# A ternary feed-forward stage: quantisation factors from the maximum alone, the inverse root on GpSimd, and another order of work on three engines

## The reference

```python
xn = layernorm(x)
def bitlinear(x, w, b):                       # w1: 1024x256, w2: 256x1024
    r = rsqrt(mean(x*x, -1) + 1e-5)           # per token
    scale = 127 / clip(max|x*r|, 1e-5)        # per token
    q = clip(round(x*r*scale), -128, 127) / scale
    wq = clip(round(w / mean|w|), -1, 1) * mean|w|
    return q @ wq.T + b
x = x + bitlinear(gelu(bitlinear(xn, w1, b1)), w2, b2)
```

## Time and profile before

| | us |
|---|---|
| median of 3 runs (lowest, highest) | 1340.75 (1338.74, 1341.14) |
| the profiled execution's own time | 1341.27 |
| its span, first to last instruction | 1339.6 |
| busy over the span: TensorE, VectorE, ScalarE, GpSimd | 1058.0, 942.7, 761.9, 224.7 |
| mean granted TensorE clock, share of full speed | 0.873 |

### The profile page before, as it was taken

How to read it: one execution, slowest core, us unless ns; L and a number is a source line. 1 busy time by engine, 2 the same in 40 slices (tenths; PEclk the granted TensorE clock), 3 DMA queues, 4 the chain that set the end, 5 groups by cost and what they waited for, 6 DMA issues and landing times. The chain is left out here.

```text
span 1339.6 us, 28328 instructions
## 1 busy us (share of the span) xinstructions
PE 1058.0 (79%) x9218; PEld 862.1 (64%) x9218; DVE 942.7 (70%) x2613; ACT 761.9 (57%) x2799; POOL 224.7 (17%) x326
## 2 busy tenths in 40 slices
PE   3999946568999823556999978999988775598885
PEld 2788843246888612445677758999977675366664
DVE  3688877755888667774677755666657984489994
ACT  1688865657888626775677762121213331488884
POOL 1233200012222101001223210000002220233431
PEclk7799968758999956776999988999998886599998
DMA  6231000000000000002322000000000000000001
GB/s 216 63 110 53 15 1 0 0 9 13 17 12 16 2 0 1 0 0 82 74 71 71 12 1 1 0 0 0 1 16 17 16 16 1 0 2 1 0 0 64
DMA packets 44421, 32.58 MB, mean 24 GB/s; under 512 B 16184, under 2 KB 43456, under 8 KB 44352
## 3 DMA queue, kind: packets, MB, share of 16 engines
q1 hardware_dynamic: 44352, 31.72, 7.8%
HBM read 23.32 MB, written 2.10 MB: 19 GB/s over the span
## 5 line engine op out<-in xcount | busy, mean ns | idle before, releaser
L680 ACT ACTIVATE L1a_pr<-L1a_scores,L1a_nm 128x128 f32<-128x128 f32 x256 | 93.1, 417 | 4.2 <-DVE L1a_nm L738 3.5
L680 ACT ACTIVATE L2a_pr<-L2a_scores,L2a_nm 128x128 f32<-128x128 f32 x256 | 90.8, 393 | 5.4 <-DVE L2a_nm L738 5.4
L680 ACT ACTIVATE L0a_pr<-L0a_scores,L0a_nm 128x128 f32<-128x128 f32 x256 | 90.8, 393 | 3.8 <-DVE L0a_nm L738 3.8
L680 ACT ACTIVATE L3f_pr<-L3f_scores,L3f_nm 128x128 f32<-128x128 f32 x256 | 90.5, 403 | 3.3 <-DVE L3f_nm L738 3.3
L680 ACT ACTIVATION_READ_ACCUMULATOR L1a_pr<-L1a_scores,L1a_nm 128x1 f32 x256 | 65.3, 255 | 0.0
L680 ACT ACTIVATION_READ_ACCUMULATOR L3f_pr<-L3f_scores,L3f_nm 128x1 f32 x256 | 62.4, 244 | 0.0
L1533 PE MATMUL L2f_inner<-L2f_taT,L2f_loraBT 128*128 128x128 f32 x512 | 59.6, 275 | 0.0
L1596 ACT COPY L2f_xTb<-L2f_xT 128x256 f32<-128x256 f32 x16 | 6.4, 406 | 93.5 <-PE L2f_inner L1522 93.5
L738 DVE TENSOR_REDUCE L2a_nm<-L2a_scores 128x4 f32<-128x512 f32 x64 | 42.2, 683 | 24.4 <-PE L2a_scores L570 24.4
L680 ACT ACTIVATION_READ_ACCUMULATOR L2a_pr<-L2a_scores,L2a_nm 128x1 f32 x256 | 59.3, 231 | 0.0
L1522 PEld LDWEIGHTS L2f_inner<-L2f_xTb,L2f_wiT 128*128 128x128 f32 x512 | 58.8, 193 | 0.4
(11 more groups left out here) (524 smaller groups left out, 3182.8 us busy)
## 6 DMA issues: line engine op xcount, KB each, us to landing
setup_ctx_nat<-in_ctx SPq DMA_DIRECT2D x4, 512.0 KB, 5.5
x_all<-in_x SPq DMA_DIRECT2D x1, 2048.0 KB, 12.4
L0a_ctxT<-ctxT_all SPq DMA_DIRECT2D x16, 128.0 KB, 2.0
L_ffn_w<-in_L_ffn_w SPq DMA_DIRECT2D x2, 1024.0 KB, 6.1
L1a_ctxT<-ctxT_all SPq DMA_DIRECT2D x16, 128.0 KB, 2.0
L2a_ctxT<-ctxT_all SPq DMA_DIRECT2D x16, 128.0 KB, 2.0
L3a_mem<-in_ctx SPq DMA_DIRECT2D x16, 128.0 KB, 2.0
out<-x_all SPq DMA_DIRECT2D x1, 2048.0 KB, 7.5
```

Of the source, the lines that this page charges most:

```text
L680: ex = act.activation(pr[q.s][:, j, h, :], S[j][:, h * P:h * P + P], ACT.Exp, bias=nm[q.s][:, j, h:h + 1], scale=-1.0, accum_out=ls[q.s][: ...
```

## The change

1. `factors` is parted. `factor` makes the scaling factor from the maximum alone (clip, reciprocal: two tiny instructions instead of five). `dequant` for the first product is one instruction with the ready root. The dequantiser of the second product moves to GpSimd.
2. The inverse root of the second product (`RsqrtPool`): VectorE makes -v/2, the shift and the first guess (four tiny instructions), GpSimd the three Newton steps (12 dependent instructions on 128x2) and the product with the kept maximum.
3. VectorE's sweep has four pairs (`sweep_four`): norm, maximum and factor 0 are made for the pair after nxt, called far. Its step now begins with max|h| and factor 1 of cur and ends with the head of cur's root; the output of old waits for GpSimd's dequantiser.
4. A quarter of hqT (second stream, second half) is written by VectorE.
5. ScalarE's order: hs of old, gelu of cur, xs of nxt, first stream's hqT of old, xqT of nxt, the third quarter of hqT, squares of cur. TensorE's order: transposes of hs of old come ahead of those of xs of nxt, and each waits for the residual of the pair before.
6. GpSimd's stream is written out for all turns without a loop.

The diff, cut to its core:

```diff
+class RsqrtPool:
+    def vector(self, dve, src, scale, eps, i):
+        dve.tensor_scalar(v, src, scale, eps, ALU.mult, ALU.add).then_inc(self.s_v, 1)
+        dve.tensor_scalar(h, src, -0.5 * scale, -0.5 * eps, ALU.mult, ALU.add)
+        dve.wait_ge(self.s_v, i)
+        dve.tensor_scalar(j, v.bitcast(I32), 1, None, ALU.arith_shift_right).then_inc(self.s_j, 1)
+        dve.wait_ge(self.s_j, i)
+        dve.tensor_scalar(y.bitcast(I32), j, -1.0, float(0x5F3759DF), ALU.mult, ALU.add).then_inc(self.s_y, 1)
+    def pool(self, pool, i):
...
+        for k in (1, 5, 9):
+            link(k, pool.tensor_tensor(t, h, y, ALU.mult))
+            link(k + 1, pool.tensor_tensor(u, t, y, ALU.mult))
+            link(k + 2, pool.tensor_tensor(t, u, self.c[:, :], ALU.add))
+            link(k + 3, pool.tensor_tensor(y, t, y, ALU.mult))
...
             def _(pool):
+                def dequant(q):
+                    pool.wait_ge(s_fac[1], q.v)
+                    if q.v > 1:
+                        pool.wait_ge(s_dq, q.v - 1)
+                    pool.tensor_tensor(am_kept[:, :], tmp[:, 1, :], dw[:, :], ALU.mult).then_inc(s_kept, 1)
+                    pool.wait_ge(rs1.s_y, q.v)
+                    r = rs1.pool(pool, q.v)
...
+                    pool.tensor_tensor(deq[:, 1, :], am_kept[:, :], r, ALU.mult).then_inc(s_dq, 1)
+                for n in range(TURNS + 1):
+                    if n < TURNS:
+                        add_b2(Pair(NS * n, n + 1))
+                    if n > 0:
+                        dequant(Pair(NS * (n - 1), n))
...
             def _(dve):
+                dve.memset(rs1.c[:, :], 1.5)
+                for s in range(NS):
+                    dve.memset(g.pad[0:1, s:s + 1], 0.0).then_inc(s_x[s], 1)
+                dve.tensor_copy(dw[:, :], wmean[:, 1:2].to_broadcast([P, NS])).then_inc(s_w2, 1)
+                def factor(q, k):
+                    dve.tensor_scalar(t, am[:, k, :], 1e-5 * 1e-5 ** 0.5, 1.0 / QMAX, ALU.max, ALU.mult)
+                    dve.reciprocal(fac[:, k, :], t).then_inc(s_fac[k], 1)
+                def dequant(q):
+                    dve.scalar_tensor_tensor(out=deq[:, 0, :], in0=tmp[:, 0, :], scalar=wmean[:, 0:1],
+                                             in1=r0[:, q.pair], op0=ALU.mult, op1=ALU.mult)
+                def step(old, cur, nxt, far):
                     if cur:
+                        if old:
+                            dve.wait_ge(s_kept, old.v)
...
+                        factor(cur, 1)
                     if old:
+                        dve.wait_ge(s_qT_ps[1][1], old.v)
+                        dve.tensor_scalar(hqT[1][:, 4:8, :], T2[1][1][:, :].rearrange("p (c t) -> p c t", c=4),
+                                          MAGIC, None, ALU.subtract).then_inc(s_qT2, 1)
+                    if far:
...
                     if nxt:
                         take_h(nxt, 0)
                         take_h(nxt, 1)
+                    if far:
...
+                        factor(far, 0)
+                        dequant(far)
                     if old:
+                        dve.wait_ge(s_dq, old.v)
...
+                    if cur:
+                        for s in range(NS):
+                            dve.wait_ge(s_sq[s], cur.v)
+                        rs1.vector(dve, ss[:, :], 1.0 / F, 1e-5, cur.v)
-                sweep_pairs(dve, step)
+                sweep_four(dve, step)
...
             def _(pe):
                 def step(old, cur, nxt):
+                    if old:               
+                        for s in range(NS):
+                            pe.wait_ge(s_scaled[1][s], old.v)
+                            pe.wait_ge(s_x[s], old.v)
...
                             pe.wait_ge(s_qT[1][s], old.v)
+                            if s == 1:
+                                pe.wait_ge(s_qT2, old.v)
```

More of the change, by code:

```diff
@@ L193, in vector, with __init__, link @@
         return y
+class RsqrtPool:
+    def __init__(self, sec, name, width):
+        self.v, self.h, self.t, self.y = (sec.sb(f"{name}_{n}", [P, width]) for n in ("v", "h", "t", "y"))
+        self.u, self.c = sec.sb(f"{name}_u", [P, width]), sec.sb(f"{name}_c", [P, width])
+        self.j = sec.sb(f"{name}_j", [P, width], I32)
+        self.s_v, self.s_j, self.s_y = sec.sem(f"{name}_v"), sec.sem(f"{name}_j"), sec.sem(f"{name}_guess")
+        self.s = sec.sem(f"{name}_newton")
+    def vector(self, dve, src, scale, eps, i):
+        v, h, y, j = self.v[:, :], self.h[:, :], self.y[:, :], self.j[:, :]
+        dve.tensor_scalar(v, src, scale, eps, ALU.mult, ALU.add).then_inc(self.s_v, 1)
[5 more added lines that the diff above has]
+    def pool(self, pool, i):
+        t, u, h, y = self.t[:, :], self.u[:, :], self.h[:, :], self.y[:, :]
+        n = 12 * (i - 1)
+        def link(k, ins):
+            ins.then_inc(self.s, 1)
+            pool.wait_ge(self.s, n + k)
+        for k in (1, 5, 9):
[3 more added lines that the diff above has]
+            link(k + 3, pool.tensor_tensor(y, t, y, ALU.mult))
+        return y
 class Pair:
@@ L216, in sweep_pairs, with sweep_four @@
     step(pairs[-1], None, None)
+def sweep_four(eng, step):
+    pairs = [Pair(NS * n, n + 1) for n in range(TURNS)] + [None] * 3
+    step(None, None, None, pairs[0])
+    step(None, None, pairs[0], pairs[1])
+    step(None, pairs[0], pairs[1], pairs[2])
+    with eng.Fori(1, TURNS - 2) as i:
+        step(*(Pair(NS * (i + n), eng.snap(i + n + 1) if n >= 0 else i) for n in (-1, 0, 1, 2)))
+    for n in range(TURNS - 2, TURNS + 1):
+        step(*pairs[n - 1:n + 3])
 def banks_of(sec):
@@ L1192, in bitlinear_ffn @@
         hqT = sbs("hqT", [P, FC, P], BF16)
[L1194 to L1195 removed]
+        hp, junk = sbs("hp", [P, F]), sbs("junk", [P, F])
         am, fac, deq, tmp = (sec.sb(n, [P, 2, NS]) for n in ("am", "factor", "dequant", "tmp"))
         ss, ms, warm = sec.sb("ss", [P, NS]), sec.sb("ms", [P, NB]), sec.sb("warm", [P, 1])
[L1198 removed]
+        rs0, rs1 = Rsqrt(sec, "rs0", NB), RsqrtPool(sec, "rs1", NS)
+        am_kept, dw = (sec.sb(n, [P, NS]) for n in ("amax_kept", "wmean2"))
+        s_kept, s_dq = sec.sem("amax_kept"), sec.sem("dequant_pool")
         wsum, wmean, winv = sec.sb("wsum", [P, 2]), sec.sb("wmean", [P, 2]), sec.sb("winv", [P, 2])
[L1201 to L1202 removed]
+        s_f2, s_fac = ([sec.sem(f"{n}{k}") for k in range(2)] for n in ("scale", "factor"))
+        s_deq = sec.sem("dequant")
+        s_w2, s_qT2 = sec.sem("factors_of_w2"), sec.sem("qT_by_vector")
         s_am, s_scaled, s_qT_ps, s_qT = ([sec.per_stream(f"{n}{k}_") for k in range(2)] for n in (
@@ L1262, in _, with add_b2 @@
                 arrived(pool, g, "L1_ffn")
[L1264 to L1270, removed]
+                pool.wait_ge(s_w2, 1)
+                def add_b2(q):
+                    for s in range(NS):
+                        b = q.b(s)
+                        pool.wait_ge(ln.s_xn[s], q.v)
+                        pool.tensor_tensor(g.x[:, b, :], g.x[:, b, :], w["b2"], ALU.add).then_inc(s_bo[s], 1)
+                def dequant(q):
[5 more added lines that the diff above has]
+                    r = rs1.pool(pool, q.v)
+                    pool.wait_ge(s_kept, q.v)
+                    for s in range(NS):
+                        pool.wait_ge(s_x[s], q.v)
+                    pool.tensor_tensor(deq[:, 1, :], am_kept[:, :], r, ALU.mult).then_inc(s_dq, 1)
[4 more added lines that the diff above has]
+                        dequant(Pair(NS * (n - 1), n))
             @block.scalar
@@ L1302, in step @@
                             act.wait_ge(s_gelu[s], cur.v)
+                            if old:
+                                act.wait_ge(rs1.s_y, old.v)
                             act.activation(junk[s][:, :], hh[s][:, :], ACT.Square, accum_out=ss[:, s:s + 1]
                                            ).then_inc(s_sq[s], 1)
[L1305 to L1312, removed]
                 sweep_pairs(act, step)
@@ L1374, in step @@
                         take_h(nxt, 1)
+                    if far:
+                        for s in range(NS):
+                            dve.wait_ge(s_am[0][s], far.v)
+                        if nxt:
+                            for s in range(NS):
+                                dve.wait_ge(s_h[s][1], nxt.v)
+                        factor(far, 0)
+                        dequant(far)
                     if old:
+                        dve.wait_ge(s_dq, old.v)
                         for s in range(NS):
@@ L1391, in step @@
                 def step(old, cur, nxt):
+                    if old:
+                        for s in range(NS):
+                            pe.wait_ge(s_scaled[1][s], old.v)
+                            pe.wait_ge(s_x[s], old.v)
+                            for f in range(FC):
+                                mm = pe.transpose(T2[s][f // 4][:, f % 4 * P:f % 4 * P + P],
+                                                  hs[s][:, f * P:f * P + P], g.ident[:, :])
```

(1 more changed line is left out.)

47 lines of the change are left out of this document (29 added, 18 removed).

## The result

The changed kernel took 1310.66 us (median of 4 runs, 1310.13 to 1311.01), the kernel before 1339.84 us beside it: a ratio of 0.978 [0.977, 0.979], 29 us less. The forecast was 1312 us. The profiled execution took 1310.86 us, with a span of 1309.1 us.

The account below looks back on a forecast made before the run. The feed-forward was bound by VectorE and ScalarE waiting on each other, 14.94 us per turn; with VectorE alone at 11.0 us the stage ends 28.8 us earlier: 1340.75 - 28.8 = 1312 us, range 1307 to 1325 us.

Parts of the forecast that it names:

- The ring of VectorE and ScalarE: Ternary feed-forward: VectorE waits for ScalarE's squares, ScalarE for VectorE's scale factors; 14.94 us per turn, 2.26 us of VectorE idle.
- VectorE's sum of 10.84 us: VectorE's priced work in one feed-forward turn after the change; taken as 11.0 us with 0.16 us for handovers.
- the norm with its maxima: VectorE, feed-forward turn: norm and two maxima for the pair after the next, priced at 1.4 us.
- The rule that I cited: VectorE and GpSimd block each other through the shared port; during Newton steps at most the norm's 0.7 us is added, within spare time.
- The dequantiser of factor 0: VectorE, one instruction per turn, priced 0.46 us like the first factor instruction, which also reads a loop-indexed column.
- GpSimd's link: One dependent instruction of GpSimd's root chain: 0.35 us taken, between 0.26 and 0.68; 13 make 4.6 us, hidden in a turn.
- Rivals 2 and 3: GpSimd's chain shows every turn above 0.64 us per link (1334 us, chance 0.08); slower than before beyond 0.87 us (chance 0.04).
- The quarter, the factor, the head of the root: VectorE's per-turn prices: quarter of hqT from PSUM 0.7 us, factor 1 0.4 us, root's head of four instructions 0.8 us.
- Start and end: Feed-forward stage outside and around its 5 loop turns of 11.0 us: ends at 590.8 instead of 619.6, 28.8 us earlier.
- TensorE's order: Transposes of hs wait for the previous pair's residual, done at 10.8 to 12.5 us, wanted at 11.0 and 13.7; no cost priced.
- Rival 1: TensorE becomes the feed-forward's bound at the low clock, 12.4 us per turn with handovers; 1322 us, chance 0.14.
- Rival 4: VectorE and ScalarE still wait for each other, 2.26 us stays; 13.1 us per turn, 1324 us, chance 0.10.

Follow-up runs that it names:

- e10: Changed kernel with TensorE making the output product twice, the second overwriting the first: 1311.81 us, turn 11.3 us.
- e8: Kernel before with only the factors made from the maximum alone and the dequantiser made separately; root on VectorE, orders as before: 1333.02 us, turn 13.8 us.
- e1: Changed kernel with the Newton steps and the second product's dequantiser back on VectorE: 1319.58 us, turn 12.6 us.
- e4: Changed kernel with GpSimd's addition of b2 moved ahead of the Newton steps: 1305.83 us, turn 10.5 us.
- e2: Changed kernel with six Newton steps on GpSimd instead of three (24 links): 1311.19 us, turn 10.8 us.
- e3: Changed kernel with nine Newton steps on GpSimd instead of three (36 links): 1332.32 us, turn 12.45 us.
- e9: Changed kernel with TensorE in its old order, transposes of xs ahead of those of hs: 1319.52 us, turn 11.4 to 13.7 us.

## Why the prediction was right, and where it was not

- **The bound and its end.** Right. The ring of VectorE and ScalarE opened, no wait for squares is left, and VectorE alone sets the turn (93% busy; 1.9 us more of TensorE in e10 change nothing). The turns order the parts: 14.94 us, 13.8 with the factors alone (e8), 12.6 with the orders, the quarter and the pair taken ahead (e1), 10.5 with the Newton steps on GpSimd and no collision (e4), 11.31 in the change.
- **VectorE's sum of 10.84 us, taken as 11.0.** The term that failed is the norm with its maxima: 552.04 - 549.92 = 2.12 us against 1.4. Everything else together came out 0.24 us shorter than its terms (11.32 - 2.12 = 9.20 against 9.44), so without the collision the turn would be 10.6 us; e4 measured 10.5. The 0.72 us of difference is the norm standing beside GpSimd's addition of b2, which had followed the norm and now runs beside it, for GpSimd is busy with the Newton steps until 549.90. I had priced the overlap of Newton steps and norm on GpSimd's side and put nothing on VectorE's. I also asked only where the new GpSimd work falls, not where it pushes the old. e1, e2 and e4 each move the addition off the norm by another edit, and each has the norm at 0.73 us; so have e3 and e9.
- **The rule that I cited.** The Trainium skill ("Advanced Engine Details and Errata", section "Mode Summary" of "VectorE Performance Modes") says that the two engines block each other through the shared second port. The runs agree that it can be either: here it is VectorE that pays (1.55 us for 0.73), and GpSimd hardly (1.46 us for 1.40). I had read it as a price on GpSimd alone. In the rows the one that starts second pays. The addition starts 0.07 us ahead of the norms in the turn shown (549.85 and 549.92), and both are long; where the first norm started ahead of it (516.37 and 516.49) only the second was, 1.14 us together; and in the earlier trace rows VectorE's product started ahead, 1188.73 and 1188.84, and the addition paid.
- **The dequantiser of factor 0, 0.46 us.** Wrong reading of a row: it takes 0.22 us (555.21). I had put the 0.46 us of the earlier trace rows on the loop-indexed column. e8 shows the same place with an operation that reads no such column: 0.54 us, ending at 543.76 as GpSimd's addition ends (543.73), while the dequantiser that does read the column takes 0.22. In the turn of the earlier trace rows it is the same: the 0.46 us end at 564.11, GpSimd's addition, whose row follows, at 564.09. So the trace of before held the collision already, and would have given the missing price.

```profile
562.69 1.40 POOL L1269 TENSOR_TENSOR x_all<-x_all,L_ffn_b 128x256 f32 x2 [13.53 <-DVE L1f_xn L164]
```

- **GpSimd's link, 0.35 us between 0.26 and 0.68.** It is 0.275 us; twelve links and the product end 3.5 us after the start, and 5.7 us stay free. Rivals 2 and 3 needed 0.64 and 0.87 us. The small-tile row (0.26 us) was the better guide, better than my 0.35 us.
- **The quarter, the factor, the head of the root.** The quarter (0.67 us) and factor 1 (0.38 us) as priced. The head takes 0.56 us instead of 0.8 (557.09 to 557.65): its first two instructions start 0.06 us apart, not 0.19.
- **Start and end.** The first step with an older pair came at 513.05 (513.4), the five turns took 56.0 us (55.0), the step without a norm 9.48 (8.7: it waits 0.82 us for the hidden matmuls and 0.55 for gelu, which I left out), the last two 11.45 together (13.7, since the chain is shorter). Of the waits of 1 to 4 us for the dequantiser that I expected in each of the last two steps only one came, 1.1 us in the last. These errors nearly cancel, 589.98 against 590.8; that the time came out within 1.4 us of 1312 is in part luck.
- **TensorE's order, valued at nothing.** The forecast needed it, but its text gave TensorE slack (transposes "wanted at 11.0 by ScalarE and 13.7 by VectorE") that holds only because the transposes of hs start at the residual, before xs is there. e9 measures that: 9 us. Rival 1 needed the transposes at the low clock on the path: in e9 they are (3.62 us, and both readers wait). In the turn shown of the change they started at 544.91 and took 2.77 us, and neither reader waited for them; in other turns ScalarE did, up to 1.4 us, and VectorE did not, so the turn stayed.
- **Rival 4** (13.1 us per turn) did not come: VectorE waited for gelu once, 0.55 us.

## What to carry to other kernels

Moving a tiny dependent chain from a full engine to an idle one pays although each link is slower (0.275 us for 0.195), as long as the result is wanted much later; how slow a link may be follows from the turn. But follow the work that the target engine already had: it shifts, and it can fall on an instruction of the full engine that it lengthens (here 4.8 us of the time, e4). And where a tiny instruction takes three times its usual time in a row, look at what the other engine does in that moment before blaming its operands.

## What was not expected of the hardware

- GpSimd's addition of two 128x256 tiles in SBUF doubles VectorE's 128x256 tensor_scalar beside it when it starts first (0.73 to 1.55 us for two), and holds a 128x2 one until it ends (0.17 to 0.51 us in e2, 0.54 in e8). Maxima over SBUF (0.74 us) and instructions that read PSUM (2.72 us) beside it keep their times (e4).
- The effect is weak the other way: the addition takes 1.40 to 1.60 us wherever it stands in this stage (the longest where a norm started just ahead of it, 1.59 us at 516.49), and a 128x2 product on GpSimd beside the norm 0.35 instead of 0.20 us (e4).
- The twelve links of GpSimd beside VectorE's maxima run at one pace, 0.20 us of work and 0.07 us between, and lengthen none of them.
